# Second transformer block: attention output made token-major with its sums, scaled once, turned by TensorE, and four products in column tiles of 32 rows

## What is computed

```python
def attention(xw, w_qkv, b_qkv, w_proj, b_proj):
    qkv = jnp.einsum('bhwc,cd->bhwd', xw, w_qkv) + b_qkv
    qkv = qkv.reshape(Bw, N, 3, HEADS, HEAD_DIM)        # N = 64 tokens, 6 heads of 16
    q, k, v = (qkv[:, :, 0], qkv[:, :, 1], qkv[:, :, 2])
    q = q * (1.0 / jnp.sqrt(jnp.float32(HEAD_DIM)))
    attn = jax.nn.softmax(jnp.einsum('bnhd,bmhd->bhnm', q, k), axis=-1)
    out = jnp.einsum('bhnm,bmhd->bnhd', attn, v).reshape(Bw, h, w, DIM_OUT)
    return jnp.einsum('bhwc,cd->bhwd', out, w_proj) + b_proj

xn = layernorm(x, g1, b1)
x = shortcut + window_unpartition(attention(window_partition(xn, 8), ...))
h = layernorm(x, g2, b2)
h = jax.nn.gelu(jnp.einsum('bhwc,cd->bhwd', h, w_fc1) + b_fc1, approximate=False)
return x + jnp.einsum('bhwc,cd->bhwd', h, w_fc2) + b_fc2
```

## Time and profile before

| | |
|---|---|
| device time, median of 3 runs | 7320.16 us (7315.06 to 7320.9) |
| span of the profiled execution | 7322.4 us |
| mean granted TensorE clock | 0.988 |
| busy share of the span | PE 96%, PEld 74%, DVE 86%, ACT 86%, POOL 75% |

### The profile page before, as it was taken

The page is one execution under the profiler, slowest core; times in us unless marked ns, Lnnn a source line. Parts: engine busy times, 40 slices in busy tenths (PEclk is TensorE's granted clock), DMA queues, the critical chain, the costliest instruction groups (busy, mean ns, idle before and its releaser), DMA issues. The chain is left out here.

```text
span 7322.4 us, 312543 instructions
## 1 busy us (share of the span) xinstructions
PE 7021.7 (96%) x110894; PEld 5453.8 (74%) x110894; DVE 6310.8 (86%) x13114; ACT 6294.8 (86%) x11444; POOL 5480.1 (75%) x6349
## 2 busy tenths in 40 slices
PE   6999999999999999999999995999999999999998
PEld 4777777777777777777777774777777777777777
DVE  5888888888888888888888885888888888888886
ACT  5999999999998999999999995877887877877877
POOL 3777777777777777777777775777777777777776
PEclk9999999999999999999999997999999999999999
DMA  0111111111111111111111111111111111111111
GB/s 21 29 30 30 30 29 30 29 29 30 30 30 29 30 30 29 30 30 30 29 30 30 30 26 27 44 44 44 44 44 44 44 44 43 44 44 44 45 44 36
DMA packets 367610, 252.62 MB, mean 34 GB/s; under 512 B 271816, under 2 KB 347336, under 8 KB 366152
## 3 DMA queue, kind: packets, MB, share of 16 engines
q1 hardware_dynamic: 366154, 233.04, 12.4%
HBM read 78.64 MB, written 77.07 MB: 21 GB/s over the span
## 5 line engine op out<-in xcount | busy, mean ns | idle before, releaser
L879 POOL TENSOR_TENSOR swin_score<-swin_score,swin_top 113x588 f32<-113x588 f32 x1024 | 1203.1, 1175 | 744.2 <-DVE swin_top L751 743.5
L622 ACT ACTIVATE swin_probT<-swin_ps_probs 128x339 f32<-128x339 f32 x2048 | 922.0, 450 | 198.7 <-PE swin_ps_probs L479 177.4
L479 PE MATMUL swin_ps_probs<-swin_ident,swin_prob 113*128 113x113 f32 x6144 | 991.8, 270 | 6.7 <-ACT swin_probT L622 6.7
L1564 POOL TENSOR_TENSOR plain_prob<-plain_prob,plain_inv_total 128x384 f32<-128x384 f32 x784 | 634.4, 830 | 450.1 <-DVE plain_inv_total L1477 450.1
L479 PEld LDWEIGHTS swin_ps_probs<-swin_ident,swin_prob 113*128 113x128 f32 x6144 | 667.9, 141 | 355.1 <-issue 320.7
L746 DVE TENSOR_TENSOR swin_score<-swin_ps_scores,swin_bias_tab 113x588 f32<-113x588 f32 x1024 | 777.9, 760 | 175.1 <-PE swin_ps_scores L469 173.8
L751 DVE TENSOR_REDUCE swin_top<-swin_score 113x12 f32<-113x588 f32 x1024 | 769.0, 751 | 0.2
L628 ACT ACTIVATE swin_prob<-swin_score 113x588 f32<-113x588 f32 x1024 | 719.0, 702 | 5.8 <-POOL swin_score L879 2.9
L782 DVE SCALAR_TENSOR_TENSOR swin_x<-swin_y,swin_y_rstd,swin_x_res 98x96 f32<-98x96 f32 x1024 | 601.7, 645 | 0.8 <-POOL swin_y_rstd L897 0.7
L1289 PE MATMUL plain_ps_dense<-plain_w_fc,plain_hid 128*128 128x96 f32 x4704 | 589.1, 275 | 2.2 <-ACT plain_hid L1362 2.2
L493 PEld LDWEIGHTS swin_ps_mixed<-swin_probT,swin_v_heads 128*32 128x32 f32 x24576 | 422.3, 109 | 222.2 <-issue 145.7
(11 more groups left out here) (188 smaller groups left out, 20880.6 us busy)
## 6 DMA issues: line engine op xcount, KB each, us to landing
swin_k_heads<-swin_k_hat SPq DMA_DIRECT2D x1024, 36.8 KB
plain_x_in<-between_blocks SPq DMA_DIRECT2D x784, 48.0 KB, 2.2
plain_k_heads<-plain_k_hat SPq DMA_DIRECT2D x392, 96.0 KB, 2.1
out_dram<-plain_x SPq DMA_DIRECT2D x784, 48.0 KB
swin_x_in<-in_x SPq DMA_DIRECT2D x224, 136.5 KB
between_blocks<-swin_x SPq DMA_DIRECT2D x224, 136.5 KB
swin_x_in<-in_x SPq DMA_DIRECT2D x224, 19.5 KB
between_blocks<-swin_x SPq DMA_DIRECT2D x224, 19.5 KB
```

The lines of the kernel that those rows point to most:

```text
L479: last = nc.tensor.transpose(psP[:, n * QT:(n + 1) * QT], prob[0:QT, p, 2 * hp:2 * hp + 2, :].rearrange('p h k -> p (h k)'), ident[0:QT, 0 ...
L622: nc.scalar.activation(to, psP[:, 0:3 * QT], ACT.Copy).then_inc(did['probT'], 1)
L879: nc.gpsimd.tensor_tensor(view, view, bcast(top[0:QT, p % 2, :], 2, WIN), ALU.subtract).then_inc(did['shifted'], 1)
L1564: nc.gpsimd.tensor_tensor(pair, pair, bcast(inv_total[0:QT, p // 2, p % 2 * heads:(p % 2 + 1) * heads], 2, WIN), ALU.mult).then_inc(did['p ...
```

## The change

In the second block only:

- v_heads no longer spreads a head's values over 32 columns of a band. For a window and a pair of heads it holds 34 columns: 16 values of the even head (non-zero only for that head's key rows), 16 of the odd head, and two columns of ones, each for one head's key rows. The ones are written once, in set-up.
- mix takes probT as the stationary operand, 32 tokens at a time, and the 34 columns of v_heads as the moving one. psO is then token-major and holds the attention output of unscaled exponentials and, in the last two of each 34 columns, their sums. There are 48 products instead of 24, in four column tiles of 32 instead of three.
- total (DVE) and scale_probs (POOL) are gone; turn_probs waits for the exponentials. scale_mixed (DVE) takes the reciprocals of the sums out of psO and multiplies psO with them into mixed, in SBUF. turn_mixed (PE) turns mixed into psT with four transposes, and copy_mixed (ACT) copies psT into mixedT.
- values, project and output are cut into column tiles of 32 rows (32, 16 and 48 products instead of 16, 4 and 12); output is one step instead of two halves.
- low_x reads x from psT instead of from xT in SBUF. psT is now used by turn_x, turn_x1 and turn_mixed, with waits for its last readers.
- Orders. PE: turn_x1 stands where turn_x stood, turn_x behind output, turn_mixed at the end of the body. ACT: high_x1 behind spread_values, then exponentials(0,2) and (0,3), then copy_x and high_x; copy_mixed behind the last gelu. DVE: scale_mixed between shift(0,2) and shift(0,3). POOL: power_x1 and norm_x1 first.

```diff
@@ -969,8 +970,7 @@
-    HB = J // 2
-    SUMS = 2 * HALF * 2
+    V = 2 * D + 2
@@ -1013,13 +1013,13 @@
-        v_heads = sb('v_heads', [128, 2, WINDOWS, BANDS, HB, 32])
+        v_heads = sb('v_heads', [128, 2, WINDOWS, HP, V])
...
-        total_of = sb('total', [128, 2, 2 * heads])
-        inv_total = sb('inv_total', [128, 2, 2 * heads])
+        inv_total = sb('inv_total', [128, PAIRS * HP, 2])
+        mixed = sb('mixed', [128, PAIRS, DIM])
@@ -1039,8 +1039,8 @@
-            part = v_heads[odd * HALF:odd * HALF + WIN, buffer, 0, 0, 0, odd * D:(odd + 1) * D]
-            return bass.AP(part.tensor, part.offset, [list(part.ap[0]), [HB * 32, WINDOWS * BANDS], [32 + 2 * D, HB], [1, D]])
+            part = v_heads[odd * HALF:odd * HALF + WIN, buffer, :, :, odd * D:(odd + 1) * D]
+            return part.rearrange('r w n d -> r (w n) d')
@@ -1108,6 +1108,10 @@
                         step(nc.vector.tensor_copy(by_turns(w_turns[:, side]), heads_apart(w_qkv[0:DIM, side])))
+                    for odd in range(2):
+                        for buffer in range(2):
+                            ones = v_heads[odd * HALF:(odd + 1) * HALF, buffer, :, :, 2 * D + odd]
+                            nc.vector.memset(ones.rearrange('r w n -> r (w n)'), 1.0)
                     dve.wait_ge(s_mul, 1)
@@ -1232,16 +1236,25 @@
                             pe.wait_ge(did['probT'], upto(g + d, PAIRS - 1, PAIRS))
+                            pe.wait_ge(did['mixed'], upto(g + d - 1))
+                            for p in range(PAIRS):
+                                for hp in range(HP):
+                                    for rows in range(0, TT, 32):
+                                        last = nc.tensor.matmul(psO[rows:rows + 32, (p * HP + hp) * V:(p * HP + hp + 1) * V], probT[:, p, hp, rows:rows + 32], v_heads[:, parity(d), 2 * p + rows // HALF, hp, :], start=True, stop=True)
+                            last.then_inc(did['mixed_made'], 1)
+
+                    def turn_mixed(d):
+                        if exists(g + d, groups):
+                            pe.wait_ge(did['mixed'], upto(g + d))
+                            pe.wait_ge(did['xT_low'], upto(g + 2))
                             pe.wait_ge(did['mixedT'], upto(g + d - 1))
-                            for w in range(WINDOWS):
-                                p, half = divmod(w, 2)
-                                for band in range(BANDS):
-                                    last = nc.tensor.matmul(psO[32 * band:32 * band + 32, w * WIN:(w + 1) * WIN], v_heads[:, parity(d), w, band, 0, :], probT[:, p, band, half * HALF:half * HALF + WIN], start=True, stop=True)
-                            last.then_inc(did['mixed_made'], 1)
+                            for p in range(PAIRS):
+                                last = nc.tensor.transpose(psT[0:DIM, p * TT:(p + 1) * TT], mixed[:, p, :], ident[0:TT, 0:TT])
+                            last.then_inc(did['mixed_turned'], 1)
 
...
                         if exists(g + d, groups):
-                            pe.wait_ge(did['prob_scaled'], upto(g + d, p, PAIRS))
+                            pe.wait_ge(did['prob'], upto(g + d, p, PAIRS))
                             ug, us = before(g + d, p, 1)
@@ -1264,15 +1277,18 @@
                                     cols = w_qkv[:, 2 * DIM:3 * DIM].rearrange('c (h o d) -> c h o d', o=2, d=D)[:, :, odd, :]
-                                    out = psM[odd * HALF:odd * HALF + WIN, bank, w * HP * D:(w + 1) * HP * D]
-                                    last = nc.tensor.matmul(out, xT[:, parity(d), w * WIN:(w + 1) * WIN], cols, start=True, stop=True)
+                                    for part in range(2):
+                                        rows = odd * HALF + 32 * part
+                                        first = w * WIN + 32 * part
+                                        last = nc.tensor.matmul(psM[rows:rows + 32, bank, w * HP * D:(w + 1) * HP * D], xT[:, parity(d), first:first + 32], cols, start=True, stop=True)
                             last.then_inc(did['v_made'], 1)
...
                             for p in range(PAIRS):
-                                last = nc.tensor.matmul(psM[0:TT, bank, p * DIM:(p + 1) * DIM], mixedT[0:DIM, parity(d), p * TT:(p + 1) * TT], w_proj[0:DIM, :], start=True, stop=True)
+                                for rows in range(0, TT, 32):
+                                    last = nc.tensor.matmul(psM[rows:rows + 32, bank, p * DIM:(p + 1) * DIM], mixedT[0:DIM, parity(d), p * TT + rows:p * TT + rows + 32], w_proj[0:DIM, :], start=True, stop=True)
                             last.then_inc(did['proj_made'], 1)
@@ -1281,20 +1297,20 @@
 
-                    def output(d, h, bank):
+                    def output(d, bank):
                         if exists(g + d, groups):
                             pe.wait_ge(did['hid'], upto(g + d, CHUNKS - 1, CHUNKS))
-                            for p in (2 * h, 2 * h + 1):
+                            for p in range(PAIRS):
                                 for c in range(CHUNKS):
-                                    last = nc.tensor.matmul(psM[0:TT, bank, p * DIM:(p + 1) * DIM], hid[:, c, p * TT:(p + 1) * TT], w_fc2[:, c, :], start=c == 0, stop=c == CHUNKS - 1)
-                            if h == 1:
-                                last.then_inc(did['fc2_made'], 1)
+                                    for rows in range(0, TT, 32):
+                                        last = nc.tensor.matmul(psM[rows:rows + 32, bank, p * DIM:(p + 1) * DIM], hid[:, c, p * TT + rows:p * TT + rows + 32], w_fc2[:, c, :], start=c == 0, stop=c == CHUNKS - 1)
+                            last.then_inc(did['fc2_made'], 1)
 
...
                             pe.wait_ge(did['x_norm'], upto(g + d))
-                            pe.wait_ge(did['x1T_low'], upto(g - 4))
-                            pe.wait_ge(did['xT'], upto(g + d - 1))
+                            pe.wait_ge(did['x1T_low'], upto(g - 3))
+                            pe.wait_ge(did['xT_low'], upto(g + d - 1))
                             for p in range(PAIRS):
@@ -1302,7 +1318,7 @@
                             pe.wait_ge(did['x1_norm'], upto(g + d))
-                            pe.wait_ge(did['xT'], upto(g + 2))
+                            pe.wait_ge(did['mixedT'], upto(g - 2))
                             pe.wait_ge(did['x1T_low'], upto(g + d - 1))
@@ -1318,13 +1334,12 @@
                     free(('k_hat', 1), ('hid', -4, 1, CHUNKS), ('x2', -5), ('v_heads', 0))
                     values(1, A)
-                    turn_x(2)
+                    turn_x1(-3)
                     free(('q_hat', 1), ('hid', -4, 2, CHUNKS), ('x1', -3))
                     project(-2, B)
                     free(('v_heads', 1), ('k_hat', 1), ('hid', -4, 1, CHUNKS), ('x2', -5))
-                    output(-4, 0, A)
-                    turn_x1(-3)
-                    output(-4, 1, A)
+                    output(-4, A)
+                    turn_x(2)
                     free(('x1', -2), ('q_hat', 1), ('hid', -4, 2, CHUNKS))
                     hidden(-3, 0, B)
@@ -1333,6 +1348,7 @@
                     free(('hid', -3, 0, CHUNKS), ('x1', -2), ('q_hat', 1), ('hid', -4, 2, CHUNKS))
                     hidden(-3, 2, B)
+                    turn_mixed(-1)
                 run_groups(pe, groups, 36, body)
 
@@ -1369,9 +1385,9 @@
-                            act.wait_ge(did['mixed_made'], upto(g + d))
+                            act.wait_ge(did['mixed_turned'], upto(g + d))
...
-                            nc.scalar.activation(mixedT[0:DIM, parity(d), :], psO[0:DIM, 0:NT], ACT.Copy).then_inc(did['mixedT'], 1)
+                            nc.scalar.activation(mixedT[0:DIM, parity(d), :], psT[0:DIM, 0:NT], ACT.Copy).then_inc(did['mixedT'], 1)
@@ -1379,7 +1395,7 @@
-                                made = psM[rows, bank, 0:WINDOWS * HP * D].rearrange('r (w n d) -> r w n d', n=HB, d=D)
+                                made = psM[rows, bank, 0:WINDOWS * HP * D].rearrange('r (n d) -> r n d', d=D)
@@ -1399,19 +1415,19 @@
                     copy_turned(-1, 3)
                     exponentials(0, 1)
-                    copy_mixed(-1)
                     spread_values(1, A)
+                    high_x1(-3)
+                    exponentials(0, 2)
+                    exponentials(0, 3)
                     copy_x(2)
                     high_x(2)
-                    exponentials(0, 2)
-                    exponentials(0, 3)
-                    high_x1(-3)
                     act.preload_act_table_set(GELU_SET)
                     gelu(-3, 0, B)
...
                     copy_turned(0, 1)
                     gelu(-3, 2, B)
+                    copy_mixed(-1)
                     act.preload_act_table_set(EXP_SET)
                 run_groups(act, groups, 36, body)
@@ -1468,13 +1484,15 @@
-                    def total(d, h):
-                        if exists(g + d, groups):
```

(33 more changed lines are left out.)

3 lines of the change are left out of this document (2 added, 1 removed).

## The result

The changed kernel takes 8083.1 us (median of four, 8072.8 to 8088.4) against 7320.5 us (7315.1 to 7321.6): a ratio of 1.104 (1.103 to 1.106), 763 us more where 149 were forecast. Its profiled execution spans 8070.9 us, 748.5 more than the one of before. The direction was right; most of the size was not seen.

What follows compares the result with a forecast made beforehand. Bound: the PE-ACT-PE round trip with two table loads, not PE's busy share. Two round trips, 14.78 and 14.8 to 14.95 us, gave 14.85 a group against 14.09; x 196 = +149 us, 7470 us; range 7400 to 7600.

Steps and rivals of the forecast that it cites:

- the longer round trip: PE to ACT and back, once a group: 14.85 us instead of 14.09, 0.76 more, +149 us in all.
- Move (a): turn_x goes behind all of output; copy_x, high_x and the GELU load follow, with gelu 0 and turn_probs(0,1) waiting behind.
- the hole: PE idle ahead of turn_probs(0,1) while ACT copies, loads the GELU table and runs gelu 0: about 1.8 us.
- The prices of the narrow tiles: Mix, values, project and output priced mainly by columns: 4.50 us (4.2 to 5.5) a group instead of 5.64.
- scale_mixed and xT_low: DVE steps: scale_mixed adds 0.79 us (reciprocal 0.23, product 0.56); xT_low falls from 1.35 to 0.69.
- The relief that finds no waiter: Work removed from DVE and POOL gives no time, since neither's total was the bound and turn_probs waited for ACT.
- Bundles of tiles show no other limit yet.: Reason for pricing mix at 0.90 us, near the column price, rather than 1.48 by starts.
- Rival 2: Feed or entry costs of the tiles: four products take 5.5 us, +335 us, 7655; chance 0.12 beyond the own range.
- Rival 3: Narrow-tile starts no closer than 21.3 ns: products 6.1 us, 16.4 a group, +453 us, 7773; chance 0.03.
- Rival 1: Faster: ACT's GELU load runs during the wait for turn_x, 13.6 us a group, -98 us, 7222; chance 0.08.
- Wrong if mix takes over 1.2 us: Sign against the forecast in PE's mix, which was expected to take about 0.9 us.
- hidden 0 still waits for x1T_low: Sign against the forecast: PE's hidden 0 would still be held up by DVE's x1T_low; no size given.

Runs made afterwards that it cites:

- e3: Changed kernel with 18 unused products filling PE's idle time ahead of turn_probs(0,1): 7897.7 us, ratio 1.079.
- e7: Changed kernel with the 18 unused products ahead of turn_probs(0,1) and values, project and output at full width: 7752.0 us, ratio 1.059.
- e5: Changed kernel with ACT's GELU table load moved ahead of copy_x and high_x: 7621.8 us, ratio 1.041.
- e6: Changed kernel with the GELU load moved ahead of copy_x and high_x, and values and project at full width: 7361.4 us, ratio 1.006.
- e8: Changed kernel with 18 unused products ahead of turn_probs(0,1) and 14 more between mix and values: 7991.1 us, ratio 1.092.
- e1: Changed kernel with values, project and output back at full width, mix still narrow: 7921.2 us, ratio 1.083.
- after: The changed kernel itself, with the whole change, against the kernel before: 8083.1 us, ratio 1.104.
- e4: Kernel before the change with only project and output in column tiles of 32 rows: 7292.4 us, ratio 0.9965.
- e9: Kernel before the change with only output in column tiles of 32 rows: 7306.3 us, ratio 0.9982.

## Why the prediction was right and wrong

**The balance of a group**, in us: 14.24 before (14.10 with its share of loop ends); + 0.75 for the longer round trip (14.85 with 0.14 for loop ends, 14.99); + 2.28 for the stops (e3's 17.28, less 0.01 of filling, less 14.99); + 0.96 for the clock; = 18.23. The round trip's term is the forecast's own, which e7 supports with 14.86, and the stops' term is what is left over, so that the sum comes out proves nothing. But the stops' term can be read in another way: in e3_warm the means of values, turn, project and output lie 0.98, 0.07, 0.29 and 0.86 above their undisturbed times, 2.20 together (over all groups, 2.15). The 3.99 more of 18.23 over 14.24, x 196, would be 782 us; the span grew by 748.5, and the stretch read (5000 to 7100) stands for the whole block within that.

**Right.**
- *What bounds the kernel.* A round trip between PE and ACT, with two table loads on it, and no engine's busy share. PE's share fell from 96% to 90% while the time rose by 10%.
- *Move (a) as the main cost.* The GELU load behind high_x made the hole (1.90 us; 1.8 to 1.9 forecast), and e5 shows that this one position costs 461 us, some two fifths of it through the clock, which the forecast did not have.
- *The prices of the narrow tiles*, undisturbed: mix 0.88 (0.90 forecast), values 0.82 (0.80), project 0.68 (0.73), output 2.12 (2.07); 4.50 in all. That this is exactly the 4.50 of the sum is luck in part: the four errors, of up to 0.05, cancel.
- *scale_mixed and xT_low.* The view of lines by form of the changed kernel, 5500 to 7000:
```profile
L1535 DVE TENSOR_TENSOR plain_xT_low<-plain_ps_turn,plain_xT_high 96x512 fp32r<-96x512 f32 x83 | 57.0, 687 | 15.3 <-ACT plain_xT_high L1412 6.5 <-DVE plain_stats L1519 0.5
...
L1495 DVE TENSOR_TENSOR plain_mixed<-plain_ps_mixed,plain_inv_total 128x384 f32<-128x384 f32 x82 | 45.7, 557 | 2.8
L1492 DVE RECIPROCAL plain_inv_total<-plain_ps_mixed 128x24 f32<-128x24 f32 x82 | 24.4, 297 | 0.0
```
  The product took 0.557 us (0.56 forecast), xT_low 0.687 (0.69), the reciprocal 0.297 (0.23 taken, 0.2 to 0.4 bounded).
- *The relief that finds no waiter.* DVE went to 73% and POOL to 60% of the span, and nothing came of it. (About 70% and 50% were forecast. In 5500 to 7000 they are busy 10.6 and 7.6 us a group, which is 71% and 51% of the forecast group of 14.85 us and less of the real one. The prediction's 0.23 us is that of a reciprocal of total; a reduction of total takes 0.94 in the kernel before, which no sum of the forecast uses.)
- *The length of the round trip*, 14.85: 14.86 by subtraction from e7. No group of the changed kernel shows it bare, since each carries clock or stops; it is supported, not seen.

**Wrong.**
- *"Bundles of tiles show no other limit yet."* This is the step that failed first. The forecast priced the four products each by itself, from rows in which a bundle stands between slower work (the earlier trace rows has 24 starts in 0.37 us, then longer ones). It never added up how many instructions follow one another: 584 in 5.07 us, where the kernel before had 96 + 64 + 8 + 16 + 24 = 208 in 4.8 (6004.21 to 6008.99 of the earlier trace rows). The page's own instruction queue, 15.30 MB in 7322 us, stood there to be asked. In its place the runs showed stops at packet ends, 2.2 to 2.3 us a group, some 430 us.
- *Rival 2* named "feed", but put it at most at 15.4 ns a start, the upper bound of the sum (+1.0 us, 7655). A bound by a price for each start cannot hold a limit of another kind: its real size was +2.2, and it came in lumps of up to 2.8 us. The chance of 0.12 and the range's upper end of 7600 followed from that.
- *The hole was priced as time and nothing else.* The prediction had the 1.9 us idle and the clock at 0.99 next to one another and did not ask what the clock does when PE idles once a group. The kernel before has no such hole: its longest in the earlier trace rows is 0.46. It costs 0.96 us a group, 185 us by e3; it had no rival and no term.
- *Rival 3*, 21.3 ns a start (7773), is closer to the measured time than the forecast and still wrong: mix makes 96 starts in 0.88 us, 9.2 ns each.
- *Rival 1* (faster, the load does not count) had the right switch and the wrong position: the load did wait behind high_x. With the load put where the rival had assumed it, the round trip falls as it said (13.5): e6's 13.97 less 0.53 for its wider values and project is 13.44. But the stops keep e5 4.1% slower than before.
- *"Wrong if mix takes over 1.2 us" and "hidden 0 still waits for x1T_low"* did not happen. Two of the other marks failed: "starts of two scores rows 14.7 to 15.0 apart" (18.23 on average) and "output about 2.1 from start to start" (3.02 in the group above, 2.89 on average, since stops fall into it). The second points at where time is lost, neither at why.

**Open.** Why a stop ends 2.5 us after a packet's start, when the packet itself is on record for 0.9 to 1.6 us (1.1 in the median), was not taken apart; whether other DMA traffic lengthens it wasn't tried. That the stops follow the supply rests on their places, 256 instructions or a multiple apart, the steady distance and e8. Why stops of up to 2.9 us, one or more in each group of e5, leave the clock at 0.97, where the hole of 1.90 us takes it to 0.89, is not shown. Nor is it shown how much the stops and the hole make each other worse: e1 and e7 differ by 169 us with wide products, after and e3 by 185 with narrow ones, so not by much.

## What to carry to other kernels

Count the instructions of the densest stretch, not only their starts times a price: the same narrow tiles lost time here in a stretch of 115 instructions a microsecond (undoing them in e1 gave 162 us back) and gained a little in one of 64 (e4). A hole on TensorE that comes once in every round is to be priced twice, as idle time and as clock for what stands behind it (0.96 us a group here). An instruction without an input, as a table load, belongs ahead of the wait on its engine and not behind it: one line was worth 461 us.

## What the runs showed of the hardware that was not expected

- Instructions come to PE in packets of 16,384 bytes, 256 instructions by the distances of the stops (148 of 151 in after are exact multiples). Where PE uses a packet up in less than about 2.6 us, it stops at its end, until 2.47 us (2.22 to 2.90) after the start of a packet's record; e8 has stops behind packets that lasted 2.7 to 3.8 us, too. Where no 256 instructions took less than 4.1 us (e9 and the kernel before) there is none.
- Starts of column tiles come closer than any rate in the rows of before: 96 starts of 34 columns in 0.88 us, 9.2 ns each (15.4 in the earlier trace rows). The floor of about 25 ns that the Trainium skill's page "TensorE: Matmul & The Clock Gate" gives (in "Wait — 56ns, not 53.3ns?"), which the prediction weighed, doesn't hold for tiles side by side. The same page's Part 3, on packing, lets them start a few nanoseconds apart. This trace is nearer to that: half of the starts of mix come within 7 ns of the one before, and the mean is 9.2.
- An idle time of 1.90 us in every group of 16 to 20 us takes the granted clock to 0.89 and the scores behind it from 1.05 to 1.93 us in more than half of the groups; one of 0.48 us does not (e5: 0.97, scores 1.05). Filling the hole with unused products, 2.07 us of them from start to start, lengthens nothing and gains 185 us.
